# A layer with attention and feed-forward: the feed-forward part of each block placed in its own iteration, runs of products joined, three buffers of exponentials, reciprocals of a turned row

## What is computed

```python
xn = layernorm(x)
# attention: 16 heads of 16 channels, 2 groups of keys and values
q = rotate(xn @ wq + bq) * 16**-0.5
k = rotate(xn @ wk + bk);  v = xn @ wv + bv
scores = einsum('bqhd,bkhd->bhqk', q, k_expanded) * 16**-0.5
attention = (softmax(scores) @ v_expanded) @ wo + bo
# feed-forward, 1024 wide
hidden = fwht(silu(xn @ W1.T) * (xn @ W3.T))
out = x + attention + hidden @ W2.T
```

## Time and profile before

| | us |
|---|---|
| median of 3 runs | 1303.58 |
| lowest and highest | 1293.02, 1316.16 |
| the profiled execution | 1307.79 |
| its span, first to last instruction | 1305.6 |
| TensorE busy in the span | 1125.1 |
| VectorE, ScalarE, GpSimd busy | 827.6, 711.4, 351.6 |
| granted clock of TensorE, mean | 0.904 |

### The profile page before, as it was taken

How to read it: one execution, slowest core, us unless ns; L and a number is a source line. 1 busy time by engine, 2 the same in 40 slices (tenths; PEclk the granted TensorE clock), 3 DMA queues, 4 the chain that set the end, 5 groups by cost and what they waited for, 6 DMA issues and landing times.

```text
span 1305.6 us, 16047 instructions
## 1 busy us (share of the span) xinstructions
PE 1125.1 (86%) x6048; PEld 538.3 (41%) x6048; DVE 827.6 (63%) x860; ACT 711.4 (54%) x1320; POOL 351.6 (27%) x300
## 2 busy tenths in 40 slices
PE   2276899978998899988998899978998999998985
PEld 1243454543444444443444434444444344533322
DVE  3766547666676657667676767667766667656611
ACT  2123347654674557654774557655774467544561
POOL 1836503205241053305241053105330013100000
PEclk9698899988998989999998999989999699977675
DMA  6330012000120022100120022000200011000001
GB/s 201 102 106 1 3 62 84 22 20 20 54 76 22 23 93 69 36 19 23 56 73 21 24 94 84 21 22 25 70 22 26 10 41 46 21 21 9 9 9 41
DMA packets 44796, 58.08 MB, mean 44 GB/s; under 512 B 11184, under 2 KB 26416, under 8 KB 44720
## 3 DMA queue, kind: packets, MB, share of 16 engines
q1 hardware_dynamic: 41408, 52.34, 13.7%
q10 hardware_dynamic: 3312, 4.72, 1.0%
HBM read 33.95 MB, written 13.63 MB: 36 GB/s over the span
## 4 chain that ended last, share of the span: by engine, by line
PE 73%; DVE 15%; issue 6%; POOL 2%; ACT 2%; ACTq 1%; SPq 0%; DMA 0%; POOLq 0%
PE ps L963 27%; PE ps L983 14%; PE ps L1067 14%; PE ps L1054 14%; DVE negpart L832 8%; PE ps L993 3%; DVE recips L863 2%; DVE y L869 1%; DVE y L814 1%; DVE stats L788 1%; PE ps L999 1%; DVE mturned L858 1%; ACTq L648 1%; DVE xnt L799 1%; DVE mturned L856 1%
## 5 line engine op out<-in xcount | busy, mean ns | idle before, releaser
L832 DVE TENSOR_REDUCE negpart<-ps 128x2 f32<-128x1024 f32 x512 | 626.5, 1225 | 388.8 <-PE ps L983 388.1
L709 ACT ACTIVATE work<-ps 128x512 f32<-128x512 f32 x1024 | 553.2, 598 | 396.1 <-PE ps L1054 391.0
L983 PE MATMUL ps<-kb,qh 48*128 48x512 f32 x1024 | 253.6, 480 | 106.5 <-DVE negpart L832 28.7
L1067 PE MATMUL ps<-work,vb 128*32 128x512 f32 x2048 | 301.3, 663 | 1.3 <-ACT work L709 1.2
L1054 PE MATMUL ps<-qh,kb 50*128 50x512 f32 x1024 | 271.9, 493 | 11.2 <-ACT work L709 11.2
L983 PEld LDWEIGHTS ps<-kb,qh 48*128 48x128 f32 x1024 | 105.8, 199 | 323.9 <-issue 139.7
L963 PE MATMUL ps<-xnt,w_p 128*128 128x512 f32 x768 | 218.4, 421 | 10.5 <-DVE negpart L832 6.5
L1054 PEld LDWEIGHTS ps<-qh,kb 50*128 50x128 f32 x1024 | 112.1, 200 | 147.5 <-issue 67.8
L963 PEld LDWEIGHTS ps<-xnt,w_p 128*128 128x128 f32 x768 | 138.3, 193 | 82.6 <-issue 49.9
L585 POOL TENSOR_TENSOR hid_p<-hid,hid_p 128x512 fp32r<-128x512 f32 x64 | 83.3, 1302 | 203.0 <-ACT hid_p L700 203.0
L581 POOL TENSOR_TENSOR hid<-hid 128x512 f32<-128x512 f32 x64 | 82.3, 1286 | 188.4 <-ACT hid L696 188.4
(11 more groups left out here) (104 smaller groups left out, 458.4 us busy)
## 6 DMA issues: line engine op xcount, KB each, us to landing
qh<-qk_parts SPq DMA_DIRECT2D x192, 64.0 KB, 2.1
y<-in_x SPq DMA_DIRECT2D x8, 512.0 KB, 4.2
recips<-osum SPq DMA_DIRECT2D x128, 32.0 KB, 2.0
attnt<-osum SPq DMA_DIRECT2D x128, 32.0 KB, 2.0
out<-y SPq DMA_DIRECT2D x8, 512.0 KB, 2.8
xn<-in_x SPq DMA_DIRECT2D x7, 512.0 KB, 3.9
qk_parts<-qe SPq DMA_DIRECT2D x14, 256.0 KB, 2.4
qk_parts<-xn SPq DMA_DIRECT2D x14, 256.0 KB, 2.4
```

Of the source, the lines that this page charges most:

```text
L709: nc.scalar.activation(prob[j % 2][:, h, :], ps[:, 4 + u % 3, :], ACT.Exp, scale=SCALE).then_inc(exp_done, 1)
L832: nc.vector.tensor_reduce(negpart[a][:, f, :, h, t, e], two(slot), AX.X, ALU.max, negate=True).then_inc(ring_free[slot], 1)
L983: m = pe.matmul(bank[:, r, :], qh[2 * q + f][rows, h, t * P:(t + 1) * P], kb[i % 2][rows, e * 512:(e + 1) * 512], start=True, stop=True)
L1067: m = pe.matmul(ps[VW * h:VW * (h + 1), 7, :], vb[b % 2][g][:, kt, :], prob[j % 2][:, h, :], start=(kt == 0), stop=(kt == ST - 1))
```

## The change

- The feed-forward part of block i moves from iteration i-1 to iteration i. The opening has none of it, iteration 7 has that of block 7. The weight products `W2` become main entries of periods 2 and 3 of iteration 0.
- The turned block, needed two iterations later, is stored in DRAM and loaded again into one pair of buffers `xf`.
- The row strings give way to an order for each kind of period. A period with an `MT` or `VT` entry (p = 2, 3, 6, 10, 14) has a kind of its own ("UPx", "DNx", "WOx", "W2x"), in which the main entry's pieces stand together. ScalarE's and VectorE's lists are written to match.
- Three buffers of exponentials instead of two.
- The denominators of 8 heads go as 8 rows of 512 to DRAM, come back as 128x32, get their reciprocal, go to DRAM again and are read back with eight broadcasts to 16 partitions each. `recips` has one buffer instead of two.
- The statistics of block i+3 are taken one tile in each of periods 8 to 11; its normalisation is split over periods 13 and 14. Its load is issued earlier.

```diff
     if p in (2, 3):
-        return ("WO", i - 1, p - 2) if i > 0 else ("DN", 0, p - 2)
-    if 4 <= p < 12 and i + 1 < NBLK:
-        return ("UP", i + 1, p - 4)
-    if p >= 12 and i + 1 < NBLK:
-        return ("DN", i + 1, p - 12)
+        return ("WO", i - 1, p - 2) if i > 0 else ("W2", p - 2)
+    if 4 <= p < 12:
+        return ("UP", i, p - 4)
+    if p >= 12:
+        return ("DN", i, p - 12)
...
+        if kind == "UP":
+            extra(); scores(0); first(0); sums_before(); first(1); scores(1)
+            own(0, 1); first(1); scores(2); own(2, 3); first(1); scores(3); sums(i, 2 * p)
+        elif kind == "DN":
+            own(0); scores(0); first(1); sums_before(); own(1); first(1); scores(1)
+            own(2, 3); first(1); extra(); scores(2); sums(i, 2 * p); scores(3); first(1)
+        elif kind == "XT":
+            first(1); first(1); own(0); scores(0); extra(); sums_before(); own(1)
+            first(1); scores(1); first(1); scores(2); scores(3); sums(i, 2 * p)
+        elif kind == "QK":
+            scores(0); first(1); sums_before(); scores(1); first(1); own(0); scores(2)
+            own(1, 2, 3); first(0); first(1); scores(3); sums(i, 2 * p); extra()
+        elif kind == "UPx":
+            first(0); scores(0); first(1); scores(1); own(0, 1, 2, 3); scores(2)
+            first(1); sums_before(); first(0); scores(3); sums(i, 2 * p); extra()
+        elif kind == "DNx":
+            own(0, 1, 2, 3); scores(0); first(1); sums_before(); first(0); scores(1)
+            first(1); scores(2); first(0); sums(i, 2 * p); scores(3); extra()
+        elif kind == "WOx":
+            first(0); scores(0); first(1); own(0, 1, 2, 3); first(1); scores(1)
+            sums_before(); scores(2); first(0); scores(3); extra(); sums(i, 2 * p)
...
-    for c in range(HC):
-        for n in range(3):
-            piece(("S1", 0, 0, 3 * c + n), 0, 1 if n < 2 else 0)
-            for k in (2 * n, 2 * n + 1):
-                if n < 2:
-                    piece(("UP", 0, c), k, 0)
-        if c == HC - 2:
+    for u in range(LEAD):
+        piece(("S1", 0, 0, u), 0, (u + 1) % 2)
+        if u == STEPS + 1:
             piece(("MT", 0, 0, 0), 0, 1)
...
+            def turn_sums(i, f):
+                sp.wait_ge(sums_out[f], 32 * (i + 1))
...
+                sp.dma_start(dens[f][:, :], sums_rows[f].rearrange("h (g n) -> (h g) n", g=HD)).then_inc(dens_in[f], 16)
+
+            def spread_recips(i, f):
+                sp.wait_ge(recip_done[f], i + 1)
...
+                sp.dma_start(recip_rows[f].rearrange("h (g n) -> (h g) n", g=HD), dens[f][:, :]).then_inc(recip_out[f], 16)
+                sp.wait_ge(recip_out[f], 16 * (i + 1))
+                for h in range(2 * QUAD):
+                    sp.dma_start(recips[HD * h:HD * (h + 1), :],
+                                 recip_rows[f, h].partition_broadcast(HD)).then_inc(recips_in, 16)
...
                 if i > 0:
                     move_sums(i - 1, 3)
+                if token:
+                    store_turned(i + 2)
+                if i > 0:
+                    turn_sums(i - 1, 1)
+                    spread_recips(i - 1, 1)
                 if token:
                     swap_keys(i + 2)
                 place_maxima(i, 0, 1)
...
                 move_sums(i, 2)
+                turn_sums(i, 0)
                 if after:
+                    load_turned(i + 1)
                     load_queries(i + 1, 1, 0)
+                spread_recips(i, 0)
+                if after:
                     place_maxima(i + 1, 0, 0)
...
-                nc.vector.reciprocal(recips[:, f, :], recips[:, f, :]).then_inc(recip_done, 1)
+                nc.vector.reciprocal(dens[f][:, :], dens[f][:, :]).then_inc(recip_done[f], 1)
```

652 lines of the change are left out of this document (458 added, 194 removed).

## The result

| | before | after |
|---|---|---|
| median, runs of one comparison | 1308.87 (4 runs) | 1224.81 (4 runs) |
| lowest and highest | 1293.02, 1316.16 | 1219.80, 1226.59 |
| ratio to before | | 0.9428 [0.9344, 0.9511] |
| the profiled execution | 1307.79 | 1226.59 |
| its span | 1305.6 | 1224.8 |

The median of the kernel before is not the 1303.58 given above because a fourth run, 1314.16, was timed beside the changed kernel.

What follows compares the result with a forecast made beforehand. TensorE was taken to bound the iterations (71.8 of 73.5 us busy), so gains lie elsewhere. Terms -20 - 28 - 33.5 - 8.4 (iteration 6) + 2 + 5.7 = -82.2 gave span 1223.4 and forecast 1222 us, range 1192 to 1258.

Steps and rivals of the forecast that it cites:

- Opening: Before the first score: without block 0's up groups only VectorE's maxima bound it, first score at 98.5, -20 us (14 to 24).
- Iteration 0: Its first four periods become usual ones, 41 us for 62.4 (-21), the other twelve give -7: -28 us (-20 to -34).
- Iterations 1 to 5: Steady iterations: seven terms sum to -6.7 us each, -33.5 in all, with bounds of -1 and -11 each.
- Small reciprocals and statistics: Steady iterations: 128x32 reciprocals and spread statistics make period 14 like 15, mean -5.3 us; second reciprocal, ahead of period 2, -1.0.
- Down and output periods: Steady iterations: fewer waits for maxima behind down sums (-2.0 us, net of an added run) and behind output sums (-2.0).
- Longer runs: Periods 6, 10, 14, 2 and 3 put their pieces into one run: -0.8 us per steady iteration.
- Period 0: Start of steady iterations: two same-slot maxima products wait (+2), early ScalarE copies delay scores (+1.5, against 1.4 idle): +2.1 us.
- The sums' way through DRAM: Steady iterations: 9.5 us from reciprocal to GpSimd's multiply delays output product and period 5's ScalarE: +2.3 us (0 to +6).
- iteration 7: Last iteration: gets block 7's feed-forward work, 39 us of TensorE, and wins back the clock: +2 us (-8 to +15).
- Tail: After the last iteration: sums' copy to multiply takes 15.4 us through DRAM against 9.7 before: +5.7 us.
- A smoother clock: Rival, whole kernel: steady iterations reach -11 us, iteration 7 -8, iteration 0 -34; span 1183, halfway 1200; chance 0.15.
- New waits eat the gain: Rival, steady iterations: SyncE/GpSimd chain +6, period 0 +4, slow stretches 1.5 per gap; 1251 to 1255 us; chance 0.15.

## Why the prediction was right, and where its terms were not

**What bounds it** held. Periods 4 to 12 of iteration 4 keep TensorE busy for 72.35 of 72.80 us at a clock of 1.00, periods 5 to 12 take 65.0 us where they took 64.9, and what was won and lost lies outside of them.

**Opening** (-20, measured -23.7; first score 94.8 for a forecast of 98.5). VectorE was the chain, and its steps were shorter than taken:

```profile
59.88 18.20 DVE L1120 TENSOR_REDUCE negpart<-ps 128x2 f32<-128x1024 f32 x16 [2.36 <-PE ps L1292]
...
82.70 1.19 DVE L523 TENSOR_TENSOR y<-work 128x1024 f32<-128x1024 f32 x1
83.81 1.22 DVE L524 TENSOR_TENSOR y<-work 128x1024 f32<-128x1024 f32 x1
```

Back to back a maximum takes 1.14 us (18.20 / 16), not the 1.21 behind the forecast's 29 us: -1.7 for 24. (The forecast's own row, 2.36 for two, gives 28.3 and not 29.) A half of the third stage takes 1.2 here, not the 2.28 of the one row that was at hand, so 2.4 for 4.2: -1.8. In the kernel before GpSimd was at work on products of 128x512 at that time, two of which took 3.46 us where one takes 1.3 elsewhere; here it has only operations of 4 columns. That they slow each other is the likely reason, and no run isolates it.

**Iteration 0** (-28, measured -16.4, outside of -20 to -34). The step that failed is the 41 us for its first four periods. They take 47.3, at a clock of 0.70, and the other twelve 104.0, 1.3 less than before instead of 7:

```profile
94.80:142.10 47.30, 40.87 (x162) 18.52 (x161) 20.15 (x20) 21.67 (x38) 21.54 (x17) 0.70 0.16 55
142.10:246.10 104.00, 99.47 (x589) 49.54 (x585) 71.81 (x83) 68.50 (x127) 25.70 (x22) 0.98 0.23 61
```

The forecast gave the slow clock 3.7 us over the steady 37.3. An opening at a clock of 0.50 (60.0 to 94.8) leads into periods with gaps of their own, and the clock is 1.00 for good only from 147.5, late in period 4. The other twelve periods miss by 5.7: period 14 gives 8.2, but 2.7 goes back in period 4, 1.8 in period 13 and 2.4 in period 15. Filling the opening did not bring the clock, so whether a warm start would mend this stays open.

**Iterations 1 to 5** (-6.7 each, measured -4.5). Taken one by one:
- *Small reciprocals and statistics*: -6.3 was forecast; alone in the old kernel they take 5.9 from period 14, as forecast, but -4.5 from an iteration on average. The term for the second reciprocal (-1.0) gave nothing: periods 1 and 2 of iteration 4 take 19.7 us with and without it. Period 11, which has a tile's statistics, takes 0.3 more, and the rest goes back in slow stretches of periods 1, 3 and 4 (clocks of 0.78 in period 1 of iteration 1, 0.95 and 0.72 in periods 3 and 4 of iteration 4). In all they give -33 to -38 us, in the two profiles with -19.7 in iteration 7, which comes back to a fast clock with them. The long reciprocal put back into the changed kernel costs 51. The mechanism was right: a 128x32 reciprocal takes 0.34 to 0.35 us, and no wait of over 1 us stands behind it.
- *Down and output periods* (-4.0). Period 14 went to 6.6, below the 9 that was forecast. But period 13, with three runs and the last products of its neighbours, takes 10.5, and period 15 12.2. Together periods 12 to 15 went from 41.1 to 37.4, where the forecast for reciprocal and down periods had -7.8. The old orders with small reciprocals take 35.2 there, and the new ones with period 0 mended 33.0, or 34.0 with the runs split: the down orders gave 1.2 of their 2.0 and the joined run 0.9, and the waits of period 0's list hide both. The output periods 2 and 3 went from 18.0 to 16.2, as forecast.
- *Longer runs* (-0.8): -0.5 by the periods at a clock of 1.00, nearly all of it from the down period, and nothing by the times. That the joined runs, which the title names second and the prediction calls first, are worth least of what was given a gain was right. So was the reading of the rows that a change of tiling costs nothing visible beyond what every new run costs: a price that matters would have shown when joined runs were split or added. Joining takes two runs out of the down period for 0.9 us, and in the up periods it costs, so no run here shows one.
- *Period 0* (+2.1): the term that failed. The mechanism was named, two products in one slot right behind another, and ScalarE's copies ahead of exponentials. Its size was not: periods 15, 0 and 1 together took 28.3 us before and take 36.8 now in iteration 4, 34 in those where period 1 is shorter, so +5.6 to +8.5 for +2.1. With another order there 37 to 41 us go, 6.2 in each of iterations 1 to 5 and 7.7 in iteration 0. The two waits were in the forecast, at +2, and measure 2.6. Missed was that the clock is 0.50 for some 14 of the 24.6 us behind them (by means of 0.68 and 0.74). The sum charged a gap with its own length only; a slow stretch behind each gap stood in a rival alone. The filled waits show that the clock's share is at least 11 us.
- *The sums' way through DRAM* (+2.3, measured 0). Each leg was shorter than forecast. Iteration 4, half 1, where period 2 begins at 693.8:

```profile
692.28 0.34 DVE L1153 RECIPROCAL dens<-dens 128x32 f32<-128x32 f32 x1
692.66 0.34 SPq L709 DMA_DIRECT2D recip_rows<-dens  x1
694.09 3.57 SPq L712 DMA_DIRECT2D recips<-recip_rows  x8
...
699.13 1.28 POOL L828 TENSOR_TENSOR attnt<-attnt,recips 128x512 f32<-128x512 f32 x1 [42.18 <-DMA recips<-recip_rows]
```

  The reciprocal starts where the forecast had it. Then come 0.34 to issue, 1.1 to land, 0.45 for each broadcast and 1.5 for the last to land: 6.5 us for 9.5. GpSimd multiplies 5.3 us into period 2, and its rotations end at 717.9, so that neither the output product nor ScalarE in period 5 waits. The error was to take the issue of a transfer and its landing from a row of another kind, `recips<-osum` at 0.62 and 2.0: the issues make up 1.6 of the 3.0 us, the two landings 1.4.
- *Third buffer* (0 against before): without it the new orders lose 11 us.

So the steady iterations got from the small reciprocals what they got in all. What the orders gained elsewhere, period 0 took away, since the same orders are worth some 3 us in iteration 4 once period 0 is mended (133.8 against 137.0).

**Iteration 6** (-8.4, measured -11.8) and **iteration 7** (+2, measured -7.3, near the bound of -8). The first two periods of iteration 6, which were in no term, take 11.5 us at a clock of 1.00, where they took 17.8 and with the old orders still take 17.9; 2.1 of that goes back in period 2. The clock of 1.00 throughout iteration 7 was forecast as over 0.85; that its first two periods, without main entries, would also be warm was left to the bound. They take 11.5 us instead of 18.2:

```profile
1079.80:1091.30 11.50, 10.73 (x67) 4.10 (x67) 9.27 (x9) 8.41 (x17) 0.00 (x0) 1.00 0.19 50
```

The reason given was wrong in part: iteration 7 was said to win the clock back by its feed-forward work. With small reciprocals alone it ran at 0.88 and took 108.1 us without that work. Seen from there the work costs 12.4 us (120.5), which is far below its 39 us of TensorE.

That a busy iteration 7 can stand at a clock of 0.68, 116.6 of 127.8 us busy, was taken from the row, and rightly: it was real and gave -7.3 back. The same is seen again in the filled opening, busy for 20.00 of 20.00 us at 0.50. No run isolates what makes the clock rise.

**Tail** (+5.7, measured +1.0). From the end of the copy to the multiply it is 11.9 us, forecast 15.4 (before, 9.7 to the reciprocal's end):

```profile
1202.63 0.59 ACT L948 COPY osum<-ps 128x512 f32<-128x512 f32 x1 [1.19 <-PE ps L1378]
...
1208.28 0.35 DVE L1153 RECIPROCAL dens<-dens 128x32 f32<-128x32 f32 x1 [2.53 <-DMA dens<-sums_rows]
...
1215.15 1.26 POOL L828 TENSOR_TENSOR attnt<-attnt,recips 128x512 f32<-128x512 f32 x1 [22.24 <-DMA recips<-recip_rows]
```

The reciprocal starts 5.1 us after the copy's end, for 5.6, and again the way behind it takes 6.5 instead of 9.5. That makes +2.2; the rest of the tail is 1.2 us shorter, which was in no step.

**The rivals.** *A smoother clock* did not come in the changed kernel (140.3 us for a steady iteration, 0.93 on average); it came with the order of period 0 mended, with a span of 1181 and a clock of 0.95. *New waits eat the gain*: they are there, in period 0 and not in the chain through SyncE and GpSimd, where they cost more than the +4 of the rival. Its 1.5 us for a stretch at 1.2 GHz behind each gap, like the lower bound of -1 for a steady iteration, rests on period 4 (9.4 us at 0.82 for runs of 7.9). A frequency no run shows; what they show is a clock of 0.71 for periods 0 and 1 of iteration 4, 24.6 us, where another order has 17.3 at 1.00. Together the clock gave more than forecast in iteration 7 and less in iteration 0, and so the sum came out right to 1.4 us by luck, for reasons that cancel: +11.6 in iteration 0 and +10.9 in the steady ones, against -3.7, -3.4, -9.3 and -4.7 in the opening, iterations 6 and 7, and the tail.

## What to carry to other kernels

When a program's order is written by hand, look at what stands on both sides of a boundary between two lists: each list may take its buffers in turn, and the last item of one and the first two of the next still want the same buffer. Charge such a wait with its own length and with the slow matmuls behind it (here at least 11 of 37 us), and look for stalls where VectorE does a long operation on rows that are copies of each other: each value once, spread over all partitions, needs a sixteenth of the columns here (3.35 us to 0.34). A sum that comes out right says little until its terms are compared stage by stage.

## What the runs showed of the hardware

- TensorE can be busy without a break and stay at a clock of 0.50: 20.00 of 20.00 us in the filled opening, and on for 27.5 us with 25.25 busy.
- The same products in the same order run at either clock: periods 0 and 1 of iteration 7 take 18.2 us in the kernel before, at 0.56, and 12.2 with small reciprocals, at 1.00. Those of iteration 6 stay slow in both, 17.8 and 17.7 us, both at 0.57.
- Of the two waits of 1.3 us ahead of iteration 4 the clock is at 1.00 up to the first one's end and falls in the second, between 666.2 and 666.4 (0.68 and 0.74 in periods 0 and 1). Four matmuls in each, which leave waits of 0.2, hold it through them; it still falls within periods 0 and 1, which run at 0.84.
- VectorE's reciprocal takes 3.35 us for 128x512, 3.34 for twice 128x240 and 0.34 to 0.35 for 128x32. The way through DRAM that makes it small takes 5.1 us ahead of it in the tail and 6.5 behind, and in the iterations no product waits for it (output products wait for GpSimd's multiply once, in the tail, 12.1 us).
